# Expert weights in one run a partition: features taken by their remainder

## The reference

```python
gu = x @ shared_gate_up_w
shared = _silu(gu[:, :Is]) * gu[:, Is:] @ shared_down_w      # Is = 1024
shared = shared * sigmoid(x @ shared_gate_w)
w, idx = top_k(softmax(x @ gate_w), 8)                       # 64 experts
buf = zeros((E, CAPACITY + 1, H)).at[e_flat, slot].set(x[tok])   # CAPACITY = 256
gu_e = einsum('ech,ehf->ecf', buf, expert_gate_up_w)         # 64 x 512 x 512
act = _silu(gu_e[..., :I]) * gu_e[..., I:]                   # I = 256
out_e = einsum('eci,eih->ech', act, expert_down_w)           # 64 x 256 x 512
```

## Time and profile before

| | us |
|---|---|
| median of 3 runs | 2779.63 (2777.95 to 2784.78) |
| the profiled execution | 2774.98 |
| its span in the profile | 2773.2 |
| PE busy | 2556.2 (92%) |
| DVE busy | 1562.3 (56%) |
| ACT busy | 1355.4 (49%) |
| POOL busy | 1340.6 (48%) |
| expert stage, first to last matmul of ex_gu | 975.6 to 1560 |

### The profile page before, as it was taken

One profiled execution on the slowest core, in us unless ns is written; L12 is line 12 of the kernel. 1 busy time (PEld: TensorE's weight loads), 2 busy tenths in 40 slices (PEclk: granted clock), 3 DMA queues, 4 the chain that ended last, 5 costly groups with the idle time before them and its releaser, 6 DMA issues. The chain is left out here.

```text
span 2773.2 us, 43616 instructions
## 1 busy us (share of the span) xinstructions
PE 2556.2 (92%) x16510; PEld 1359.4 (49%) x16510; DVE 1562.3 (56%) x2474; ACT 1355.4 (49%) x3019; POOL 1340.6 (48%) x1043
## 2 busy tenths in 40 slices
PE   6888889999999999999999978887999999999999
PEld 3333334444444377777777634443444444444444
DVE  6899976555555255565656567876543432334232
ACT  4787874222222166666666468876433222232221
POOL 4777770665555546676666457886102201121111
PEclk9999989999999999999999979998999999999999
DMA  7899986222221299999999779999410110011000
GB/s 206 163 198 182 188 160 201 62 62 62 62 62 46 91 320 273 281 291 293 278 293 278 176 147 185 197 182 201 137 39 16 46 46 31 16 46 46 23 8 31
DMA packets 602351, 389.75 MB, mean 141 GB/s; under 512 B 470048, under 2 KB 479008, under 8 KB 602144
## 3 DMA queue, kind: packets, MB, share of 16 engines
q1 hardware_dynamic: 565280, 319.64, 44.6%
q0 software_dynamic: 36864, 67.34, 11.8%
HBM read 198.86 MB, written 75.89 MB: 99 GB/s over the span
## 5 line engine op out<-in xcount | busy, mean ns | idle before, releaser
L1752 POOL DMA_INDIRECT ids<-sh_tk,sh_su x256 | 269.5, 1053 | 242.9 <-PE sh_gu L55 70.5
L2699 POOL TENSOR_TENSOR fe_prodT<-fe_pp,fe_prodT 128x512 f16<-128x512 f32 x64 | 77.8, 1216 | 590.9 <-ACT fe_prodT L2484 590.9
L55 PE MATMUL ex_gu<-ex_xT,ex_h 128*128 128x256 f16 x3072 | 345.8, 273 | 4.2 <-issue 3.4
L2151 POOL DMA_INDIRECT xp<-ex_oo,ex_to x128 | 243.2, 1900 | 181.5 <-ACT ex_oo L2059 143.3
L55 PEld LDWEIGHTS ex_gu<-ex_xT,ex_h 128*128 128x128 f16 x3072 | 300.3, 98 | 52.7 <-issue 4.3
L1886 DVE SCALAR_TENSOR_TENSOR ex_h<-ring,ex_h 128x1024 f16<-128x1024 f32 x128 | 151.1, 1222 | 158.2 <-ACT ex_h L1876 156.8
L55 PE MATMUL at_g<-hm_zT,hm_w 128*128 128x512 f16 x768 | 192.4, 406 | 19.5 <-DMA hm_zT<-hm_zs 14.8
L2615 DVE SCALAR_TENSOR_TENSOR ring<-fe_g,fe_nf,ring 128x512 f32<-128x512 f32 x32 | 24.0, 751 | 293.0 <-PE fe_g L2400 293.0
L1860 POOL DMA_INDIRECT ex_xg<-zrows,ex_idxu x128 | 155.1, 1212 | 55.6 <-issue 33.2
L55 PE MATMUL sh_g<-sh_wdn,sh_actT 128*128 128x512 f16 x768 | 171.9, 383 | 8.6 <-issue 5.4
L55 PE MATMUL ex_o<-ex_h,ex_aT 128*128 128x512 f16 x768 | 176.2, 379 | 0.0
(11 more groups left out here) (367 smaller groups left out, 5371.7 us busy)
## 6 DMA issues: line engine op xcount, KB each, us to landing
ring<-L_ffn_expert_gate_up_w SPq DMA_DIRECT2D x64, 1024.0 KB
ring<-L_ffn_expert_down_w SPq DMA_DIRECT2D x64, 512.0 KB
ring<-x SPq DMA_DIRECT2D x24, 1024.0 KB, 6.1
x<-ring SPq DMA_DIRECT2D x16, 1024.0 KB, 5.0
zrows<-hm_zs SPq DMA_DIRECT2D x32, 256.0 KB
xp<-ring SPq DMA_DIRECT2D x8, 1024.0 KB
out<-ring SPq DMA_DIRECT2D x8, 1024.0 KB, 4.3
ring<-xp SPq DMA_DIRECT2D x7, 1024.0 KB, 6.4
```

The source lines that it names most:

```text
L55: mm = nc.tensor.matmul(out, lhs(a, k), rhs(b, k), start=start and i == 0 and j == 0, stop=stop and i == n - 1 and j == 2)
L1752: e.indirect_dma_start(ids, bass.IndirectOffsetOnAxis(slotu[b % 2][:, t, j:j + 1], 0), pair[b % 2][:, t, j, :], None, bounds_check=SLOTS - ...
L2151: e.indirect_dma_start(dst, bass.IndirectOffsetOnAxis(to[:, n:n + 1], 0), o32[y % 2][:, t, :], None, bounds_check=T + SLOTS - 1, oob_is_er ...
L2699: e.tensor_tensor(prodT[:, 1, j, :], p32[q % 2][:, :], prodT[:, 0, j, :], ALU.subtract).then_inc(s["p_lo"], 1)
```

## The change

The loads of the expert weights and of the gates give partition p the neighbouring rows 4p to 4p + 3 (first layer, 512 features) or 2p and 2p + 1 (second layer, 256 hidden features), which in main memory are one run of 8 KB, 4 KB, or 1040 bytes for the gates. Step k of a product over 512 features so holds the features 4p + k, those with the remainder k by four. The norm of the shared stage (`mixed`) writes its features in that order, and the shared gate-up weights are loaded in it too (their runs stay slices of 512 columns). For the second layer the hidden features must come as 2p + a: the columns of the first layer's weights are sorted by their remainder a when they are split. ACT reads its 1024 elements with a step of two; DVE does it in two instructions of 512 for each former one.

```diff
--- before.py
+++ after.py
@@ -96,7 +96,7 @@
         self.nc, self.s, self.K, self.x, self.nx, self.nzs = nc, s, K, x, len(x), len(homes.zs)
         self.z, self.zs, self.zT = homes.z, homes.zs, [homes.zT]
 
-        self.tiles = []
+        self.tiles, self.mixed = [], False
         self.stats = sb("stats", [P, TPB, 6], F32)
         self.mv = sb("mv", [P, TPB, 2], F32)
         self.lv = sb("lv", [P, TPB], F32)
@@ -145,8 +145,10 @@
         v.wait_ge(s["rstd"], b + 1)
         if n >= 2:
             v.wait_ge(s["lo"], n - 1)
-        v.tensor_scalar(self.z[n % 2][:, :], self.block(b)[:, t, :], self.mv[:, t, 0:1], self.rstd[:, t:t + 1],
-                        ALU.subtract, ALU.mult).then_inc(s["z"], 1)
+        z, x = self.z[n % 2][:, :], self.block(b)[:, t, :]
+        if self.mixed:
+            z, x = z.rearrange("q (k p) -> q k p", k=KT), x.rearrange("q (p k) -> q k p", k=KT)
+        v.tensor_scalar(z, x, self.mv[:, t, 0:1], self.rstd[:, t:t + 1], ALU.subtract, ALU.mult).then_inc(s["z"], 1)
 
     def scalar_high(self, n):
 
@@ -1363,10 +1365,11 @@
         self.nc, self.I, self.s, self.src, self.homes = nc, I, s, src, homes
         self.x = [ring[i] for i in (3, 2, 4, 1, 0)]
         self.nrm = Norm(nc, ctx, "sh", s, K, self.x, homes)
+        self.nrm.mixed = True
         self.slots = [ring[i] for i in (4, 1, 0)]
 
         self.scat = [ctx.enter_context(nc.semaphore(f"sh_scat{i}")) for i in range(2)]
-        up = I["L0_ffn_shared_gate_up_w"].rearrange("(k p) n -> p k n", p=P)
+        up = I["L0_ffn_shared_gate_up_w"].rearrange("(p k) n -> p k n", p=P)
         down = I["L0_ffn_shared_down_w"].rearrange("(k p) n -> p k n", p=P)
         self.pieces = [up[:, :, n * 512:(n + 1) * 512] for n in range(4)] + [down[:, 4 * n:4 * n + 4, :] for n in range(2)]
 
@@ -1398,8 +1401,8 @@
 
     def sync_ahead(self, before):
 
-        self.nc.sync.dma_start(self.homes.gates32[:, :, :], self.I["gates65"].rearrange("(k p) n -> p k n", p=P)
-                               ).then_inc(self.s["wg_in"], 16)
+        self.nc.sync.dma_start(self.homes.gates32[:, :, :].rearrange("p k n -> p (k n)"),
+                               self.I["gates65"].rearrange("(p k) n -> p (k n)", p=P)).then_inc(self.s["wg_in"], 16)
         for i in range(3):
             self.nc.sync.wait_ge(*before.stored(4 + i))
             self.sync_piece(i)
@@ -1836,12 +1839,14 @@
         self.st2 = [ring[2][:, 0:2, :], ring[2][:, 2:4, :], ring[4][:, 0:2, :]]
 
     def sync_first(self, x):
-        self.nc.sync.dma_start(self.st1[x % 3][:, :, :], self.I["L0_ffn_expert_gate_up_w"][x, :, :]
-                               .rearrange("(k p) n -> p k n", p=P)).then_inc(self.s[f"w1_in{x % 3}"], 16)
+        self.nc.sync.dma_start(self.st1[x % 3][:, :, :].rearrange("p k n -> p (k n)"),
+                               self.I["L0_ffn_expert_gate_up_w"][x, :, :].rearrange("(p k) n -> p (k n)", p=P)
+                               ).then_inc(self.s[f"w1_in{x % 3}"], 16)
 
     def sync_second(self, x):
-        self.nc.sync.dma_start(self.st2[x % 3], self.I["L0_ffn_expert_down_w"][x, :, :]
-                               .rearrange("(k p) n -> p k n", p=P)).then_inc(self.s[f"w2_in{x % 3}"], 16)
+        self.nc.sync.dma_start(self.st2[x % 3].rearrange("p k n -> p (k n)"),
+                               self.I["L0_ffn_expert_down_w"][x, :, :].rearrange("(p k) n -> p (k n)", p=P)
+                               ).then_inc(self.s[f"w2_in{x % 3}"], 16)
 
     def tensor_slots(self, banks):
         self.nc.tensor.wait_ge(self.s["ids_in"], 16)
@@ -1867,13 +1872,21 @@
         for n in range(2 * self.NS):
             self.gpsimd_rows(n, zrows)
 
+    def staged_by_half(self, x, k):
+
+        return self.st1[x % 3][:, k:k + 2, :].rearrange("p k (g n a) -> p (k g) a n", g=2, a=EI // P)
+
+    def by_half(self, w1, h, k):
+
+        return w1[:, h, k:k + 2, :].rearrange("p k (g a n) -> p (k g) a n", g=2, a=EI // P)
+
     def scalar_weights(self, x, w1=None, w2=None):
         a, s, w1, w2 = self.nc.scalar, self.s, w1 or self.w1, w2 or self.w2
         a.wait_ge(s[f"w1_in{x % 3}"], 16 * (x // 3 + 1))
         if x >= 2:
             a.wait_ge(s["up_mm"], x - 1)
         for k in range(0, KT, 2):
-            a.activation(w1[:, 0, k:k + 2, :], self.st1[x % 3][:, k:k + 2, :], ACT.Copy, scale=WS).then_inc(s["w1_hi"], 1)
+            a.activation(self.by_half(w1, 0, k), self.staged_by_half(x, k), ACT.Copy, scale=WS).then_inc(s["w1_hi"], 1)
         a.wait_ge(s[f"w2_in{x % 3}"], 16 * (x // 3 + 1))
         if x >= 3:
             a.wait_ge(s["dn_mm"], self.NS * (x - 2))
@@ -1883,8 +1896,10 @@
         v, s, w1, w2 = self.nc.vector, self.s, w1 or self.w1, w2 or self.w2
         for k in range(0, KT, 2):
             v.wait_ge(s["w1_hi"], 2 * x + k // 2 + 1)
-            v.scalar_tensor_tensor(w1[:, 1, k:k + 2, :], self.st1[x % 3][:, k:k + 2, :], WS, w1[:, 0, k:k + 2, :],
-                                   ALU.mult, ALU.subtract).then_inc(s["w1_lo"], 1)
+            for a in range(EI // P):
+                low = v.scalar_tensor_tensor(self.by_half(w1, 1, k)[:, :, a, :], self.staged_by_half(x, k)[:, :, a, :], WS,
+                                             self.by_half(w1, 0, k)[:, :, a, :], ALU.mult, ALU.subtract)
+            low.then_inc(s["w1_lo"], 1)
         v.wait_ge(s["w2_hi"], x + 1)
         v.scalar_tensor_tensor(w2[:, 1, :, :], self.st2[x % 3][:, :, :], WS, w2[:, 0, :, :], ALU.mult, ALU.subtract
                                ).then_inc(s["w2_lo"], 1)
```

## The result

| | before | changed |
|---|---|---|
| median of 6 runs each, us | 2781.82 (2777.95 to 2784.78) | 2798.84 (2794.38 to 2803.83) |
| ratio, 95% interval | | 1.0062 (1.0047 to 1.0076) |
| profiled execution, its span | 2774.98, 2773.2 | 2798.51, 2796.8 |
| ex_gu, first to last matmul of the experts | 975.6 to 1560.1 | 980.4 to 1589.1 |
| experts in 1000 to 1550 us (ex_gu matmuls / 48) | 60 | 57.6 |

The change makes the kernel slower by 0.6%. I had forecast 2768 with a range up to 2790: wrong in sign, and outside the range.

The account below looks back on a forecast made before the run. PE and the DMA engines were taken to bound the expert stage neck and neck. Profiled execution 2774.98 us - 14 (cheaper weight packets) + 3 (later load issue) = 2764, plus 4.65 to the median: 2768 us, range 2757 to 2790.

Parts of the forecast that it names:

- What bounds the kernel now: Expert stage: PE (8.80 us an expert) and DMA engines (about 9.17) neck and neck; cheaper transfers gain at most 0.37 us.
- The runs of the weights: Expert weight loads: 8 KB packets at 320 ns, 4 KB at 164, saving 0.23 us an expert, 14 us in all.
- the line through two points: Packet price fitted to 2 KB at 85.5 ns and 3.4 KB at 139: 7.2 ns a packet plus 0.0382 ns a byte.
- the round without its waits: Expert stage, the round in which DVE could bind: 7.75 us against 9.17, so 0.33 us more DVE work hides.
- As q0 and q1 together fill the engines [...], what one queue saves the other gets: Expert stage's two DMA queues: the weights' saving passes to the other queue, 0.23 us x 61 experts = 14 us.
- ACT's and DVE's halves, the norm: Expert weight splits and shared-stage norm: ACT's step taken as 0, DVE's +0.33 us an expert hidden, norm taken as 0.
- DVE's issue of the next load: SP's next first-layer load, issued after DVE's low halves, moves 0.3 us back; cost taken as 0.05, 3 us in all.
- R: Experiments' theory, not the forecast's: four shorter DVE instructions let POOL's scatter precede the 8 KB load; expected ratio 1.005 to 1.015.
- Rival D: Expert stage: 8 KB packets go between the scatter's, which lands 1.4 us later; a seventh lost, +12 us, 2792; chance 0.11.
- rival B: Expert weight loads: no change, 8 KB costs four of 2 KB or the saving is lost; 2776 to 2784; chance 0.30.

Follow-up runs that it names:

- e5: Kernel before with both expert loads in runs of 4 KB, no new order elsewhere: 2783.86 us, ratio 1.0102 to the kernel before.
- e1: Kernel before with only the two expert loads changed, to runs of 8 KB and 4 KB: 2862.1 us, ratio 1.0390 to the kernel before.
- e2: Changed kernel with each expert load made by two transfers in runs of 2 KB: 2758.21 us, ratio 1.0016 to the kernel before.
- f5: Kernel before with expert loads in 8 and 4 KB runs, and DVE's first-layer low halves in four contiguous instructions, not two: 2797.65 us, ratio 1.0069.
- f2: Changed kernel with the first layer's 8 KB load issued behind the second layer's load: 2795.24 us, ratio 1.0055 to the kernel before.

## Why the prediction was wrong, by its own steps

- **"What bounds the kernel now": half right.** PE and the DMA engines run neck and neck, and a round is 9.17 us. But the engines' share of 1.02 was read as demand against capacity. The rows of before hold a third thing of the same length: the loop over the scatters, 9.11 and 9.02 us (1205.29 to 1214.40 to 1223.42), of which POOL's instructions are 4.14. ACT's 63.6 us, 55 times, were its sign; I named them and drew nothing from them.
- **"The runs of the weights", the price: right in sign, too small.** 320 and 164 ns forecast; the records have 309 and 159 (medians), and by the queue's share q1's packets cost 0.33 us an expert less in place of 0.23. The 128 packets behind the line through two points are not of one size, which the view does not tell: 108 gather packets of 4 KB, 159 ns each, and 20 of 4 bytes, 9 ns. Of less weight: the round without its waits is 7.78 us by its rows, not 7.75, and 2764 + 4.65 is 2769.
- **"As q0 and q1 together fill the engines [...], what one queue saves the other gets": this is the step that failed.** In these traces the engines serve the two queues not by bytes or by need but packet for packet. A longer packet on q1 takes from q0 at the moment both are at work and gives back later, when q0 has nothing: 14 us of gain became 24 of loss. With DVE's two instructions as before, the loss is 1.0% with 4 KB packets (e5) and 3.9% with 8 KB (e1), although these are the cheapest.
- **ACT's and DVE's halves, the norm: right.** 1132 ns in place of 1054 (bounds 1054 to 1700, taken 1054), 687 in place of 693, together worth 0.16% (e2). The norm's step of four costs less than the 0.32 us a tile that its nearest row led to expect: L148 took 537 ns at least and 723 at the median for the shared stage, and now

```profile
L151 DVE TENSOR_SCALAR hm_z<-ring,sh_mv,sh_rstd x32: 743/796/2343, 338.0 to 871.9; 128x512 f32<-128x512 f32 x32
```

  0.21 us more between the shortest and 0.07 between the medians, under a PE that is busy 100.00 of 100 us. The rule of the Trainium skill (Advanced Engine Details and Errata, SBUF Cachelines) that I cited holds for DVE: a step of two is free (687 ns with it, 687 in f5 without), a step of four pays. ACT pays 7% for its new pattern, which the rule does not say; its writes changed as well as its reads, and the two were not tried apart.
- **DVE's issue of the next load, "moves 0.3 us back ... I take 0.05": right size, wrong sign and weight.** The four instructions move the issue back by 0.67 us against the end of POOL's scatter instruction (from 0.28 before it to 0.39 after it). That is what R is about: with long packets it is worth 3% of the kernel (f5 against e1).
- **Rival D, "packets in turn": the mechanism that ran, at 0.11.** Its reckoning of one meeting was good: I had 6 of an engine's packets meet the load at 0.24 us each, 1.4 us; in e1 it is 7 (112 over 16 engines), 1.7 of the 2.07 us by which the transfer grew (4.20 to 6.27). Wrong was "the sum over both stays; only if the time in between stays empty is it lost", of which I gave a seventh: in e1 the loop grew by 2.08 us, the whole of the delay. In the full change it is lost in some rounds only, which comes to 0.38 us an expert, twice my 0.2. I judged D by the sum over two queues, the quantity that it leaves alone, in place of by who waits for the transfer.
- **The rule behind rival B (the Trainium skill, DMA: Bandwidth & Descriptors, Specifications), by which 2 KB and 8 KB cost the same:** by the rows above the weights' queue is 8% cheaper a byte (41.0 against 44.4 engine-us a MB), so the trace disagrees by that much, and the rule says nothing of the other queue, which is what counted.
- A part of the loss is PE's own work, a step that my sum lacked. It is busy 569.82 us in the expert stage, 558.87 before, 11 of the stage's 24 us: ex_o's matmuls take 386 ns in place of 379, at a granted clock of 0.99 in place of 1.00, and 411 ns at 0.96 in e1. Four microseconds of e1, 1216 to 1220 (PE busy, granted clock, DMA share, GB/s), show where:

```profile
1216.00:1220.00 4.00, 3.21 (x20) 0.61 0.83 90
```

  PE had just waited 1.99 us for a gather (until 1216.57), which the first 0.57 us of the stretch belong to; the granted clock is 0.61 of full speed on average, so most of this stretch is at 1.2 GHz, and it is 1.00 in the four before. I had counted a wait at its length only.

What stays open: why POOL's instruction ends with one of DVE's (below), and what else makes a round of the changed kernel long or short.

## What to carry to other kernels

Ask of a transfer not what share of the DMA engines it takes but who waits for it: a bulk load that is early and a small scatter that is late are not to be added up. Where two queues share the DMA engines packet for packet, as here, long runs on a queue that nobody waits for slow down the queue that somebody waits for; keep the bulk packets no longer than the urgent ones, and if the urgent ones are to go first, count what the later bulk load meets then (f2: the gathers). When a part of a change alone is worse than the whole, look for what the rest of the change does to the order of issues.

## What the runs showed of the hardware that I had not expected

- The two queues alternate packet for packet at both sizes seen: 97 packets of 2 KB beside 102 of up to 8 KB in 3 us (e1), 55 beside 51 with 2 KB each in 1 us (before).
- A packet of a scatter that adds takes 178 ns for 2 KB (median, before), a load's packet 84 ns for 2 KB, 159 for 4 and 309 for 8.
- POOL's indirect DMA instruction takes 2.22 us (before, e1) or 1.75 us (changed) for the same scatter of 128 rows; beside it DVE ran instructions of 1222 or of 687 ns. The gather behind it goes the other way, on average 1199 ns in e1 and 1530 in f5. That POOL waits for DVE at the end of its instruction fits the constant distance to an end of DVE's, 0.31 us in 56 of 59 rounds before and in 49 of 49 in e1; it wasn't tried by itself.
- A step of two float32 in ACT's input, with the output in runs of 128, costs 1132 ns against 1054 for 1024 elements; a step of two costs DVE nothing (687 ns for 512 with it and without it, f5).
